# One half of the value projection moved a TensorE slot later, one piece of the second FFN product a slot sooner, in an attention and FFN block

## The reference

```
x = x + layernorm(attention(layernorm(x)))
x = x + layernorm(ffn(layernorm(x)))
attention: q, k, v = 16 heads of 32; a query sees the 256 keys up to its own; softmax; out @ Wo.T + bo
ffn:       h = bitlinear(x, w_fc) + gate * (x @ v.T @ fast_b.T @ u.T);  bitlinear(relu(h)**2, w_proj)
```

## Time and profile before

| What | Value |
|---|---|
| Median of three executions | 2284.57 us (2282.37 to 2287.46) |
| Profiled execution: its own time | 2285.86 us |
| Profiled execution: span of the trace | 2284.1 us |
| Mean granted TensorE clock | 0.989 |
| Busy: TensorE matmul | 2191.4 us (96%) |
| Busy: TensorE weight loads (beside the matmuls) | 1655.8 us (72%) |
| Busy: VectorE, ScalarE, GpSimd | 1738.3, 1637.0, 1474.8 us |

### The profile page before, as it was taken

One profiled execution on the slowest core, in us unless ns is written; L12 is line 12 of the kernel. 1 busy time (PEld: TensorE's weight loads), 2 busy tenths in 40 slices (PEclk: granted clock), 3 DMA queues, 4 the chain that ended last, 5 costly groups with the idle time before them and its releaser, 6 DMA issues.

```text
span 2284.1 us, 61076 instructions
## 1 busy us (share of the span) xinstructions
PE 2191.4 (96%) x20149; PEld 1655.8 (72%) x20149; DVE 1738.3 (76%) x4619; ACT 1637.0 (72%) x4647; POOL 1474.8 (65%) x2570
## 2 busy tenths in 40 slices
PE   4788999999999999999999999999999999999997
PEld 3556777777777777777777777777777777777664
DVE  7887777877778877777787777888778787786764
ACT  3787776777767776777767776677767777677752
POOL 4455666776666776666667666667766667675553
PEclk9899999999999999999999999999999999999999
DMA  6333233223333323333332232332233233322211
GB/s 222 122 94 96 82 94 102 79 90 102 91 96 96 90 76 103 102 88 95 92 94 88 88 101 87 104 92 83 86 101 108 79 97 92 88 82 75 60 39 37
DMA packets 230587, 210.80 MB, mean 92 GB/s; under 512 B 34928, under 2 KB 170096, under 8 KB 229248
## 3 DMA queue, kind: packets, MB, share of 16 engines
q1 hardware_dynamic: 227584, 198.51, 29.1%
q10 hardware_dynamic: 2688, 8.39, 1.0%
HBM read 137.53 MB, written 67.17 MB: 90 GB/s over the span
## 4 chain that ended last, share of the span: by engine, by line
PE 87%; DVE 5%; ACT 4%; issue 2%; DMA 1%; POOL 1%; SPq 0%; ACTq 0%; POOLq 0%; DVEq 0%
PE Ab L634 21%; PE F L704 19%; PE F L731 16%; PE Cb L634 9%; PE Ob L624 7%; PE Tb L606 6%; PE S L590 6%; PE F L716 3%; ACT Sm L852 1%; DVE Sm L1172 1%; ACT x2T L906 1%; ACT qk L899 0%; ACT qk L897 0%; ACT PT L870 0%; DVE r L1298 0%
## 5 line engine op out<-in xcount | busy, mean ns | idle before, releaser
L870 ACT ACTIVATE PT<-Tb 128x384 f32<-128x384 f32 x896 | 440.4, 491 | 442.5 <-PE Tb L606 438.6
L1172 DVE CUSTOM_DVE_ANT_0 Sm<-S,mask,scales 128x384 f32<-128x384 f32 (+2 forms) x1024 | 572.2, 561 | 219.6 <-PE S L590 212.5
L852 ACT ACTIVATE Sm<-Sm,nmax 128x384 f32<-128x384 f32 (+2 forms) x1024 | 584.5, 571 | 108.1 <-DVE nmax L1172 106.0
L704 PE MATMUL F<-x2T,t 128*128 128x256 f16 x4096 | 489.1, 272 | 0.0
L731 PE MATMUL F<-t,r 128*128 128x512 f16 x2048 | 482.0, 379 | 1.3 <-DVE r L1298 1.2
L704 PEld LDWEIGHTS F<-x2T,t 128*128 128x128 f16 x4096 | 397.9, 98 | 52.2
L634 PE MATMUL Ab<-xT,w_attn 128*128 128x256 f16 x2928 | 366.2, 276 | 4.3 <-DVE w_attn L1026 4.3
L731 PEld LDWEIGHTS F<-t,r 128*128 128x128 f16 x2048 | 197.4, 97 | 197.4 <-DVE r L1298 1.7
L590 PE MATMUL S<-QK 96*128 96x384 f16 (+2 forms) x1280 | 316.7, 280 | 8.7 <-DVE nmax L1172 5.9
L1410 POOL TENSOR_TENSOR lnrs<-lnve,nhalf 128x1 f32<-128x1 f32 x192 | 122.6, 638 | 310.7 <-DVE lnve L1260 127.3
L634 PEld LDWEIGHTS Ab<-xT,w_attn 128*128 128x128 f16 x2928 | 282.2, 99 | 55.3 <-issue 12.6
(11 more groups left out here) (199 smaller groups left out, 3285.1 us busy)
## 6 DMA issues: line engine op xcount, KB each, us to landing
QK<-qk_hop SPq DMA_DIRECT2D x768, 64.0 KB, 2.0
qk_hop<-qkp SPq DMA_DIRECT2D x128, 256.0 KB, 2.1
x<-in_x SPq DMA_DIRECT2D x64, 256.0 KB, 2.9
x_hop<-sq SPq DMA_DIRECT2D x256, 64.0 KB, 1.8
r<-x_hop SPq DMA_DIRECT2D x64, 256.0 KB, 2.7
out<-yb SPq DMA_DIRECT2D x64, 256.0 KB, 2.2
xa<-in_x SPq DMA_DIRECT2D x30, 512.0 KB, 3.8
xa<-in_xt SPq DMA_DIRECT2D x30, 512.0 KB, 4.4
```

What stands on the lines that cost most here:

```text
L704: pe.matmul(Fb[b][:, half * STEP:(half + 1) * STEP], W["t1"][:, mc, k, :], x2T[:, part, k, :], start=(half == 0 and k == 0 and part == 0), ...
L852: act.activation(blk, blk, ACT.Exp, bias=nmax[:, hg % 2, j % 8:j % 8 + 1], scale=-1.0, accum_out=sums[:, hg % 2, j % 8:j % 8 + 1]).then_in ...
L870: act.activation(PT[:, tile % NPT].rearrange("p b n -> p (b n)"), Tb[:, 0:WIN], ACT.Exp, bias=1.0, scale=c_score).then_inc(M["T_exp"], 1)
L1172: v.tensor_tensor_reduce(Sm[:, j % NSM, c0:WIN], Sb[j % 2][:, c0:WIN], W["mask"][:, c0:WIN], W["c"][:, 3:4], 3e38, ALU.add, ALU.min, nmax[ ...
```

## The change

The first half of the values of tile 0 moves from slot 35 to 36, and piece 1 of the second FFN product of tile 1 from slot 68 to 67. In an iteration that has both, the two change places: slot 3 holds the FFN piece and slot 4 the value half. The tables of the first two steps (`V_EARLY`) are as they were.

```diff
-V_SLOT = {35: (0, 0), 37: (0, 1), 43: (1, 0), 45: (1, 1)}
+V_SLOT = {36: (0, 0), 37: (0, 1), 43: (1, 0), 45: (1, 1)}
...
-FF2_SLOT = {59: (0, 0), 60: (0, 1), 62: (0, 2), 64: (0, 3), 66: (1, 0), 68: (1, 1), 70: (1, 2), 74: (1, 3)}
+FF2_SLOT = {59: (0, 0), 60: (0, 1), 62: (0, 2), 64: (0, 3), 66: (1, 0), 67: (1, 1), 70: (1, 2), 74: (1, 3)}
```

## The result

The change is faster. Six executions of each kernel gave a median of 2276.24 us (2275.72 to 2278.86) after and 2287.06 us (2282.37 to 2287.95) before; the ratio is 0.996 with a 95% interval of 0.9947 to 0.9972, so 9 us, between 6 and 12 (10.8 between the medians). A second series of six executions of the same changed kernel, beside thirteen of before, gave 0.9965 (0.9953 to 0.9977). The profiled execution took 2275.91 us over a span of 2274.2.

A forecast was written before the change was run, and what follows sets the result against it. The prediction took TensorE's stream, with one hole per iteration, to bound the kernel. Closing 28 holes gave -10.1, the edge +0.3, so 2284.57 - 9.8 = 2274.8 us; range 2271.7 to 2281.0.

The forecast's parts named there:

- The hole and its cause: Slot 3, iterations 3 to 30: TensorE's value half waits 28 times for ScalarE's L899, late behind L906's copy.
- Its size: Slot 3 hole, start to start: 0.36 or 0.37 us, times 28 gives 10.1 us off the stream.
- The rival that trusted the idle column: TensorE's loop holes: only the visible idle comes back, 28 x 0.20 = 5.6, less 0.3, so 2279.3 us; chance 0.06.
- The FFN piece as cover, price 0: Tile 1's FFN piece, one slot sooner, waits for nothing and covers the late ScalarE copy; price 0.
- The chain I wrote down for the new slots: Slots 3 and 4 on TensorE: value half starts at 1061.30, slot 4's tile at 1062.61, 3.13 after the row shifts' issue.
- The row shifts, the rival of no change: Slot 4's tile waits for row shifts landing 3.13 to 3.49 us after issue; 0.36 becomes a new wait, 2284.6; chance 0.10.
- VectorE, the slower rival: Slots 3 to 6: VectorE becomes the bound, 28 x (0.84 - 0.36) = +13.4, 2298.0 us; chance 0.06.
- The room of 0.98: Slot 5's score block: VectorE's reading of slot 3's score block ends at 1061.80, new start 1062.78, 0.98 us left.
- The edges: Iteration 1 costs 0.3 us for the exposed value half; iteration 2 gains 0, at most 0.34; iteration 31 priced 0.
- The total: Whole run: -10.1 + 0.3 = -9.8 us, from the median 2284.57 to 2274.8; forecast chance 0.78.

The follow-up runs named there:

- the kernel that keeps iterations 1 and 2: The change, but the value halves issued in iterations 1 and 2 stay in slot 35, against the kernel before: 2277.04 us, ratio 0.9962.

## Why the prediction was right

**The hole and its cause.** One hole per iteration, made by ScalarE's L906 ahead of the bias copies: shown by exchanging the two, which closes it without the change, and by delaying them with one more copy, which widens it by 0.53, the spacing of such a copy.

**Its size.** 0.36 to 0.37 us from start to start; measured 0.371 in the loop, so 10.4 for the 28. The rival that trusted the idle column, 0.20, would have had 5.6 us and fell. The rule of the Trainium skill (page Perfetto Trace Analysis, section Tensor Engine Instruction), that the end of a matmul is estimated, agrees with the two pairs of numbers here: 0.36 against 0.20 and 0.88 against 0.72.

**The FFN piece as cover, price 0.** Beside the value half's move it costs nothing, but it is not incidental. Alone it costs 14 us, and without it the value half's move costs 10.7. The chain I wrote down for the new slots came out within 0.02 us: the value half 2.23 behind the score block of slot 3 (measured 2.22), the next tile 3.13 behind the DMA of the row shifts (1057.88 - 1054.76 = 3.12).

**The row shifts, the rival of no change.** At 3.12 us after the issue the tile did not wait. But the prediction read this margin from one iteration, and others have less. The trace of before had one already: in iteration 24 the DMA is issued at 1665.50 and the tile of slot 4 starts at 1667.65, 2.15 later and not 3.49, without a wait; 0.36 sooner it would have come before the 2.09 that the prediction took for the landing. In iteration 12 of the profile after, the tile of slot 4 starts 859.36 - 856.74 = 2.62 after the issue, and does not wait either:

```profile
856.74 0.71 SPq L437 DMA_DIRECT2D QK<-turned  x1
859.36 0.34 PE L606 MATMUL Tb<-QK 128*128 128x128 f16 x2
```

In the same iteration of the kernel that keeps iterations 1 and 2 it did wait, for this DMA (timeline of all engines; one more line in the file):

```profile
856.63 0.71 SPq L438 DMA_DIRECT2D QK<-turned  x1
857.98 1.47 PE L635 MATMUL Ab<-w_attn,xT 128*128 128x256 f16 x12
859.56 0.11 PEld L607 LDWEIGHTS Tb<-QK 128*128 128x128 f16 x2 [0.39 <-DMA QK<-turned]
```

There the tile starts 2.93 after the issue, and 1.58 after the value half instead of 1.31: 0.27 of the 0.37 was given back, once. The two kernels with more work on VectorE have the same wait in the same iteration; the two profiles of the change do not. So the rival's mechanism is real: issue and landing both vary from iteration to iteration, and the price of 0 held because the tile waits for the rows in one iteration of the loop in some profiles and in none in others. One wait in iteration 2 was thin evidence for it.

**VectorE, the slower rival.** The room of 0.98 was right in the iteration from which it was read (0.97 in the profile after), and one added operation of about 0.65 fits where two do not. The price was not its lateness over the room: I had about 0.35 per iteration for every kind of step, and they lose between 0.10 and 0.69. The rival's 0.84 was too high as a mean.

**The edges.** I charged 0.3 us for the exposed value half in iteration 1. That term was not settled: profiles of one kernel differ there by more than the term, with the clock in it (last section). It does not decide a sum of 10. For iteration 31 I had 0, and the product of its slot 8 comes 64.02 us after that of iteration 30, against 64.03 before.

**The total.** Forecast 9.8 us off; the spans of the profiled executions differ by 9.9, the ratio gives 9 and the medians 10.8. The measured median, 2276.24, is 1.4 above the forecast of 2274.8. The forecast stood on a median of before of 2284.57 from three executions; with three more it is 2287.06, 2.5 higher, and the change came out 1.0 larger by the medians. Both differences lie within the scatter of whole executions. That the total is met to about 1 us is therefore in part luck; the 0.371 per iteration of the loop is not.

## What to carry to other kernels

In a stream that is written out by hand, a late hand-over (a buffer that another engine frees late) can be covered by exchanging the waiting piece with a neighbour that waits for nothing, but the exchange has to be complete: a slot that is left with only short, chained pieces opens a larger hole than the one that was closed. Size a hole on TensorE from the start of one group to the start of the next and take off the same distance where nothing waits; the idle column left out the same 0.16 us at 0.36, at 0.51 and at 0.88. Read a margin to a DMA in every iteration and not in one. And look at what stands ahead of the late instruction on the engine that makes it late: here two lines exchanged on ScalarE were worth the same 10 us.

## What the runs showed of the hardware that I had not expected

Two like waits in iteration 1 were followed by a lower clock in one execution and not in another. The change, profiled first (TensorE, slots 3 and 4 of iteration 1):

```profile
125.92 0.34 PE L606 MATMUL Tb<-QK 128*128 128x256 f16 x2 [1.59 <-ACT PT L870]
128.01 1.01 PE L555 MATMUL Cb<-x,V 128*128 128x128 bf16 x8 [1.74 <-ACT u_T L832]
128.81 0.53 PE L590 MATMUL S<-QK 96*128 96x384 f16 x1
129.13 2.77 PE L634 MATMUL Ab<-w_attn,xT 128*128 128x256 f16 x12
131.69 0.53 PE L590 MATMUL S<-QK 96*128 96x384 f16 x1
```

The same kernel, profiled again:

```profile
127.00 0.34 PE L606 MATMUL Tb<-QK 128*128 128x256 f16 x2 [1.69 <-ACT PT L870]
129.08 0.61 PE L555 MATMUL Cb<-x,V 128*128 128x128 bf16 x8 [1.74 <-ACT u_T L832]
129.52 0.33 PE L590 MATMUL S<-QK 96*128 96x384 f16 x1
129.69 1.47 PE L634 MATMUL Ab<-w_attn,xT 128*128 128x256 f16 x12
131.00 0.33 PE L590 MATMUL S<-QK 96*128 96x384 f16 x1
```

Busy time by stretch, the first and the second profile (before the two numbers at the end, DMA share and GB/s, stands the granted clock):

```profile
126.00:128.00 2.00, 0.26 (x2) 0.06 (x3) 2.00 (x5) 2.00 (x5) 1.52 (x2) 0.78 0.01 2
128.00:134.00 6.00, 5.99 (x36) 4.62 (x37) 3.91 (x11) 4.61 (x13) 0.41 (x1) 0.51 0.35 109
```

```profile
126.00:128.00 2.00, 0.34 (x2) 0.11 (x2) 1.35 (x4) 2.00 (x7) 0.93 (x2) 1.00 0.57 234
128.00:134.00 6.00, 4.79 (x52) 4.05 (x52) 5.17 (x13) 5.78 (x15) 1.00 (x2) 1.00 0.40 112
```

Two waits of 1.6 to 1.7 and 1.74 us, with two matmuls between them, stand in both. In the first the granted clock is 0.51 afterwards, the 1.2 GHz level, and the value half takes 2.56 us (129.13 to 131.69); in the second it stays at 2.4 GHz, and the half takes 1.31. The stream ahead of the waits was not quite the same: the score block of slot 0 still ran at the lower level in the first (at 119.56, its record 0.53 long) and no longer in the second (at 120.83, 0.33 long). Why the clock fell in one only is not shown. Before has a fall of its own there, a little later: its granted clock was 0.59 and 0.56 from 136 to 138 and from 138 to 140 us.

From the weighted values of iteration 0 (117.94 us before) to the low-rank product of iteration 2 (197.02 before) the four profiles of kernels without added work that have the value half of iteration 1 in slot 36 took 77.1, 77.4, 79.5 and 81.2 us, the six that have it in slot 35 took 77.7 to 79.2. The lowest and the highest of the four are the two profiles above: one kernel, 4.0 us apart. The fall of the clock is a part of this and not all: counted from the weighted values (115.58 and 117.52), the score block ahead of the waits (124.00 and 124.98) stands 0.96 later in the first already, the one behind the value half (131.69 and 131.00) 2.63, and the rest comes after. The loop of the same two differs by less than 0.1 us.
